# Eight more products into an unread bank behind each group of the relation pass

## The reference

```python
def _L2_gnn_ref(h, W, bias_term, gate_weight, gate_bias, loop_weight, src, dst, rel):
    loop_message = h @ loop_weight
    xw = jnp.einsum('ni,rio->rno', h, W)
    msg = xw[rel, src] + bias_term[rel]
    gw = gate_weight[..., 0]
    gate = jax.nn.sigmoid(jnp.sum(msg * gw[rel], axis=-1) + gate_bias[rel, 0])
    agg = jax.ops.segment_sum(msg * gate[:, None], dst, num_segments=n_nodes)
    node_repr = agg + loop_message
    return jax.nn.relu(node_repr)

x = _layernorm(x + _L0_gnn_ref(x, edge_index, ...))   # attention
x = _layernorm(x + _L1_gnn_ref(x, edge_index, ...))   # MLP
x = _layernorm(x + _L2_gnn_ref(x, ..., src, dst, edge_type_8))
x = _layernorm(x + _L3_gnn_ref(x, edge_index, ...))   # attention
```

## Time and profile before

| | us |
|---|---|
| median of three runs | 5380.08 |
| the profiled execution | 5375.34 |
| its span, from first to last instruction | 5373.5 |
| relation pass, first to last gather start | 2856.8 to 4030.5 |
| first attention pass, the same | 51.5 to 1251.7 |
| MLP pass, the same | 1335.0 to 2547.6 |
| second attention pass, the same | 4087.9 to 5286.7 |

### The profile page before, as it was taken

The page is one execution under the profiler, slowest core; times in us unless marked ns, Lnnn a source line. Parts: engine busy times, 40 slices in busy tenths (PEclk is TensorE's granted clock), DMA queues, the critical chain, the costliest instruction groups (busy, mean ns, idle before and its releaser), DMA issues. The chain is left out here.

```text
span 5373.5 us, 52586 instructions
## 1 busy us (share of the span) xinstructions
PE 3031.7 (56%) x15318; PEld 2725.6 (51%) x15318; DVE 2583.0 (48%) x5261; ACT 1435.2 (27%) x3816; POOL 3188.7 (59%) x3353
## 2 busy tenths in 40 slices
PE   2667676666477777777663232323322566666665
PEld 2566566665466666666631232322322556655665
DVE  2354444545477777777772121111212355554555
ACT  0010010101488888888651000000000011111111
POOL 5666666662666666666015666666664666666662
PEclk6556666656798888898876566666665655555656
DMA  5333333332333333333033111121112333333331
GB/s 126 86 104 101 99 97 101 101 95 69 99 102 101 102 101 102 102 101 101 4 141 101 44 50 49 47 51 49 51 49 65 86 97 95 100 98 95 99 98 50
DMA packets 254435, 458.48 MB, mean 85 GB/s; under 512 B 105399, under 2 KB 153912, under 8 KB 254136
## 3 DMA queue, kind: packets, MB, share of 16 engines
q0 software_dynamic: 119808, 280.51, 20.3%
q1 hardware_dynamic: 127272, 169.92, 9.7%
q10 hardware_dynamic: 7056, 4.56, 0.3%
HBM read 411.70 MB, written 43.03 MB: 85 GB/s over the span
## 5 line engine op out<-in xcount | busy, mean ns | idle before, releaser
L881 POOL DMA_INDIRECT rows<-gat_table,src_i x1664 | 1576.8, 948 | 840.3 <-issue 470.5
L1561 POOL DMA_INDIRECT rows<-mlp_table,src_i x832 | 788.8, 948 | 507.1 <-issue 306.4
L1293 POOL DMA_INDIRECT rows<-rel_table,rel_i x832 | 787.0, 946 | 443.0 <-issue 298.3
L1168 PE MATMUL p_sum<-rows,hot 128*128 128x133 f32 x3328 | 783.2, 424 | 36.6 <-issue 18.3
L1160 PEld LDWEIGHTS p_adc<-adw,hot_t 128*128 128x128 f32 x3328 | 659.4, 303 | 275.8 <-DVE hot_t L919 252.1
L1160 PE MATMUL p_adc<-adw,hot_t 128*128 128x8 f32 x3328 | 658.3, 336 | 233.3 <-DVE hot_t L919 218.5
L1168 PEld LDWEIGHTS p_sum<-rows,hot 128*128 128x128 f32 x3328 | 733.0, 325 | 38.7 <-DVE rows L945 20.4
L1450 PE MATMUL p_sum<-hot,rows 128*128 128x128 f32 x1664 | 305.8, 350 | 709.1 <-DVE hot L1320 419.4
L1722 PE MATMUL p_sum<-hot,rows 128*128 128x128 f32 x3328 | 510.9, 326 | 334.3 <-issue 302.5
L1722 PEld LDWEIGHTS p_sum<-hot,rows 128*128 128x128 f32 x3328 | 490.7, 238 | 376.1 <-issue 340.1
L1450 PEld LDWEIGHTS p_sum<-hot,rows 128*128 128x128 f32 x1664 | 281.9, 260 | 734.3 <-DVE hot L1320 437.1
(11 more groups left out here) (262 smaller groups left out, 3869.0 us busy)
## 6 DMA issues: line engine op xcount, KB each, us to landing
drow<-in_dst_rows SPq DMA_DIRECT2D x208, 512.0 KB
rows<-gat_table,src_i POOLq DMA_INDIRECT x1664
rel_table<-tab SPq DMA_DIRECT2D x49, 512.0 KB, 2.6
rows<-mlp_table,src_i POOLq DMA_INDIRECT x832
eat<-in_edge_t SPq DMA_DIRECT2D x104, 128.0 KB
rows<-rel_table,rel_i POOLq DMA_INDIRECT x832
gat_table<-tab SPq DMA_DIRECT2D x23, 274.0 KB
mlp_table<-tab SPq DMA_DIRECT2D x11, 512.0 KB
```

The lines of the kernel that those rows point to most:

```text
L881: pool.indirect_dma_start(out=rows[:, n % RING, t, :], out_offset=None, in_=net.gat_table[:, :], in_offset=bass.IndirectOffsetOnAxis(ap=ne ...
L1168: end = nc.tensor.matmul(p_sum[:, 0:SUMS], hot[:, n % HALF, t, :], rows[:, n % RING, t, 0:SUMS], start=(t == 0), stop=(t == T - 1))
L1293: pool.indirect_dma_start(out=rows[:, n % RING, t, :], out_offset=None, in_=net.rel_table[:, :], in_offset=bass.IndirectOffsetOnAxis(ap=ne ...
L1561: pool.indirect_dma_start(out=rows[:, n % RING, t, :], out_offset=None, in_=net.mlp_table[:, :], in_offset=bass.IndirectOffsetOnAxis(ap=ne ...
```

## The change

A constant `FILL = 8` is added, and a PSUM tensor `p_idle`. Behind the eight products of each group, after the one that raises `summed`, PE multiplies `FILL` times the identity and one tile of the group's one-hot, each product by itself, into `p_idle`, which nobody reads. No wait and no signal is added.

```diff
+FILL = 8
@@ rel_pass
         p_iota = s.ps("p_iota", [P, P])
+        p_idle = s.ps("p_idle", [P, 512])
         px = s.ps("px", [P, UNIT, P])
@@ add_up(n) on TensorE
                 for t in range(T):
                     end = nc.tensor.matmul(p_sum[n % 2][:, 0:P], rows[:, n % RING, t, :], hot[:, n % HALF, t, :], start=(t == 0), stop=(t == T - 1))
                 end.then_inc(s.summed, 1)
+                for t in range(FILL):
+                    nc.tensor.matmul(p_idle[:, 0:P], net.ident[:, :], hot[:, n % HALF, t, :], start=True, stop=True)
```

## The result

The changed kernel takes 5406.55 us, the median of five runs (5398.31 to 5411.24), against 5380.08 for the kernel before (5378.63 to 5388.16, five runs too). The ratio is 1.0038 with an interval of 1.0027 to 1.0050: slower, by 20 us on the ratio and by 26 us on the medians. The profiled execution took 5399.78 us with a span of 5398.0; before it was 5375.34 and 5373.5. So 24.5 us of span are to be explained.

A forecast was written before the change was run, and what follows sets the result against it. The prediction took the relation pass to be bound by POOL's gathers and their debt, not the products. +14 us in the pass and +6 in the tail gave +20, forecast 5400 us (+0.37%), range 5362 to 5442 us.

The forecast's parts named there:

- What bounds the pass: Relation pass: the gathers' pace on POOL with its debt sets the time, not the products; PE idle for 70%.
- The debt line: POOL's stops beyond the usual 0.30 us: about 0.147 us for each gather of the run plus 0.45 us per stop.
- Runs of 16 in place of 32: Relation pass: with fill, POOL stops after about 16 gathers instead of 32, 52 stops in place of 30.
- +14 in the pass: Relation pass: more POOL stops cost +14 us, taken between +10 and +22; bounds -13 and +39.
- +6 in the tail: After POOL's last gather: five groups +0.9 us each, some +4.5, and the last fill +1.8; taken as +6 us.
- The clock at 0: Middle of the relation pass: denser PE work raises the granted clock from 0.62 to 0.7 or more, worth 0 us.
- (d): Rival: a faster clock shortens each of 30 catch-ups by 1.5 us, giving 5335 us; chance 0.06.
- The bank: `p_idle` in PSUM: nothing waits for it or reads it, no wait is added, 0 us.
- (a): Rival: POOL stops at every group, 1.459 us a gather, +39 us and +10 in the tail, 5429 us; chance 0.20.
- (b): Rival: all hidden in the pass, runs stay at 24 to 32, only the tail costs, 5384 us; chance 0.27.
- (c): Rival: products behind the group push its late signal out, POOL stops less; up to 134.5 us, 5246 us; chance 0.06.
- (e): Rival: unread products might vanish or the clock not rise; the latter leaves the sum as is; no chance given.

The follow-up runs named there:

- six_b: Kernel before the change with six gathers per group instead of eight in the relation pass, output wrong; first to last gather there took 890.4 us against 1173.7.
- fill2: The changed kernel with two products of fill per group instead of eight; ratio 1.0005 to the kernel before the change.
- fill16: The changed kernel with sixteen products of fill per group instead of eight; ratio 1.0128 to the kernel before the change.
- half_b: Kernel before the change with relation-pass gathers of 64 rows instead of 128, output wrong; first to last gather there took 1182.1 us.
- paced_b: Kernel before the change with two 128x1 POOL memsets ahead of each gather in all passes, no fill; 5406.3 us, ratio 1.0044.
- ring16_b: Kernel before the change, no fill, with sixteen slots instead of eight in the relation pass's ring `rows`; 5438.4 us, ratio 1.0042.
- narrow: The changed kernel with its eight fill products cut to 8 columns moved and 32 loaded; ratio 1.0032 to the kernel before the change.
- Tailoff: The changed kernel without fill behind the last eight groups; ratio 1.0022 to the kernel before the change.

## Why the prediction was right, step by step

**What bounds the pass.** Held. PE's busy time in the pass nearly doubled, and the pass is still 831 intervals of 1.25 us and the stops, 1038.8 + 149.0 = 1187.8.

**The debt line.** 0.147 us a gather and 0.45 a stop were read from stops of other passes. For after it gives 122.3 + 0.45 x 51 = 145.3 us and 149.0 were found, for six_b 110.6 and 112.8, for fill2 with its 36 true stops 138.5 and 140.1. It falls short in fill16 (155.6 for 179.0) and in half_b, whose gathers are shorter. It describes the sum well. As a rule for a single stop it doesn't hold (after 8 gathers 0.46 to 7.30 us in after), and its 0.45 for a stop fell with paced_b. The prediction read the debt as something that POOL outruns and that needs 1.397 us a gather; that this isn't the transfers is shown by the empty windows of ring16_b.

**Runs of 16 in place of 32.** Held in kind: 24 of 51 runs have 16 gathers, none has 32, and 51 waits are close to the 52 that I put. The argument was that about 64 records get through at a stop. Counting matmul records of the windows over the whole pass per wait supports it: 1696 x 1.1737 / 34 = 59 before, 2069 x 1.1774 / 42 = 58 in fill2, 3102 x 1.1882 / 51 = 72 in after, 72 in fill16, 82 in narrow, while PE's records per us rise from 1.7 to 4.4. Some waits are too short to delay a gather; by intervals over 1.35 us there are 29 stops before, 36 in fill2, 51 in after, 74 in fill16 and 46 in narrow, and the records per stop are 69, 68, 72, 72 and 80. The deeper ring, which left the runs at 32, speaks for it too, since it changes no record. It isn't exact: six_b has 49.

The Trainium skill, "TensorE: Matmul & The Clock Gate", section "Architectural detail", has the queue of 64 that I weighed. The trace doesn't bear out the size. There the prediction counted matmuls and weight loads together (32 records of fill and 32 of a group are one group of after), and counted so, 116 to 144 get through per wait in before, fill2 and after. Only the matmuls alone come near 64. No run here shows a queue as such.

**+14 in the pass.** Measured +14.5, but the working behind it is doubtful. I priced 22 more stops at 0.45, which is +10, and went up toward the runs of 16 as seen. The trace has 17 more waits, or 22 more stops if those that delay no gather are left out (51 for 29). By the debt line they are worth 7.7 or 9.9 us, half or two thirds of what was found. And paced_b shows that the number of stops isn't what is charged. The line over instructions gives 3328 more of them (1664 matmul records and as many weight loads) x 4.15 ns = 13.8 us, from rows that I had in front of me. I used the MLP and attention passes there only as bounds. So the term came out right by luck in part: the price was too small, and a guess upward mended it.

**+6 in the tail.** Measured +6.3. Timeline of PE in after's tail:

```profile
4053.04 1.95 PE L1452 MATMUL p_sum<-hot,rows 128*128 128x128 f32 x16
...
4061.87 1.95 PE L1452 MATMUL p_sum<-hot,rows 128*128 128x128 f32 x16
...
4065.88 1.95 PE L1452 MATMUL p_sum<-hot,rows 128*128 128x128 f32 x16
...
4070.39 1.95 PE L1452 MATMUL p_sum<-hot,rows 128*128 128x128 f32 x16
...
4074.28 1.95 PE L1452 MATMUL p_sum<-hot,rows 128*128 128x128 f32 x16
```

The groups here are 4.0, 4.5 and 3.9 us apart where I had 2.7 before, so each is +1.2 to +1.8, not +0.9. There are also six of them, not five, and they begin 4.0 us after POOL's last gather (4049.0), not 8.9. The last real record starts 27.0 us after POOL's last gather, where it was 22.6. That is +4.4, as my +4.5 for the groups, but it is the sum of an earlier start, one more group and dearer groups. So the size of this term is luck in part too. Tailoff, with 55.5 us, shows that the tail's growth goes away with the fill of the last eight groups.

**The clock at 0.** The direction was right and the size too small in one place. I expected a granted clock of 0.7 or more in the pass, and it rose from 0.62 to 0.68; at 0.76, in fill16, the kernel is slowest. The stops got no shorter with it, so rival (d) is out: after 24 gathers 4.58 us against 4.35. In the tail the clock is worth something, by narrow's 3.78 against 1.95 us for one group. I had left that out because the tail looked warm before, in a window of 2.5 us; its first two groups took 6.44 us where after's take 1.95 and 2.05.

**The bank.** 0, as put: no wait in after names `p_idle`.

**The rivals.** (a), a stop at each group, is what fill16 approaches (53 runs of 8, 1.465 us a gather), not eight products. (b) is excluded by the stretch of +14.5 and by the ring. (c), that the signal only lacks work behind it, is refuted on all four bases: with more behind each group the waits rose (34 to 51, 30 to 46, 31 to 51, 29 to 48). (d) see above. (e) is out: 3102 records in place of 1696.

**The signs I named.** More than 34 waits: 51. Last gather 10 to 25 us later: 18.5, or 14.5 from the same start. Stops after 16 at about 3.3: 24 of them, 18 within 3.1 to 3.4 us and the others from 1.0 to 2.5. Records doubled. Clock at 0.7: missed, 0.68. None of the three signs against it appeared, but the one on stops after 32 gathers couldn't, as after has no run of 32; in fill2 the nine of them are 5.6 us and more.

**What stays open.** What charges 0.16 us to each gather beyond its 1.25, why an instruction of any engine adds to it, and why PE's records come singly for most of a run. The page shows how instructions are supplied, as packets of a DMA queue; these are its rows of before and of after:

```profile
q8 instruction: 128, 2.10, 0.2%
...
q8 instruction: 141, 2.31, 0.2%
```

With the fill's 3328 instructions there are 13 more packets of 16 KB, and 26 more in fill16 (154). Such a supply would fit the cost of an instruction. But it doesn't explain the debt itself: in the long stop of ring16_b the DMA engines are at 0.00 for 17 us, and POOL still waits. So a supply that the engines share with the gathers remains argued, and the late signal is one more thing that it would have to account for.

## What to carry to other kernels

Filler on an engine that is idle 70% of the time isn't free: here each product that nobody reads cost some 17 ns (14.5 us / 832) of the pass that another engine bounds, and the higher clock that it bought was worth nothing in the pass, where the stops go by the gathers. Before warming an engine, look in the waits for a row that a shorter product would end sooner. And where several passes share one bound, put their pace against their instructions: here a line through two passes of the kernel before gives the changed one within 0.5 us, better than a count of its stops, though it was drawn only afterwards and misses other kernels by 3 us and more.

## What the runs showed of the hardware

- Indirect gathers from POOL start every 1.25 us but keep up only one per 1.41 over a pass. Halving their rows took the instruction from 0.947 to 0.901 us and left 32 of them at 45.32 us with their stop, against 45.36.
- What POOL waits for in a stop isn't data: in ring16_b's stop of 23.11 us all engines are idle and the DMA share is 0.00 for 17 us, and the add that starts at 3110.40 belongs to a product whose records are over by 3030.5.
- Behind a stop some sixty PE records run back to back, 16 in 1.95 to 3.62 us, while POOL already issues gathers again (3444.02 in after). Then they come singly, 0.7, 1.4 or 2.1 us apart with nothing waited for (3464.56, 3466.65), until 4 us into the next stop.
- The 0.30 us between two gathers hides one memset of 0.12 us or two of 128x1 on the same engine (interval 1.25 to 1.26). With two, POOL pauses by itself, up to 1.51 us with nothing waited for.
- Instructions of any engine beside streaming gathers cost some 3 to 5 ns each of their pace, PE's and POOL's alike (fitted to the passes, above).
- An fp32 product of 32 loaded and 8 moved columns took 0.04 us a record where the granted clock was 1.00 (16 in 0.67) and 0.06 where it was 0.50 (16 in 1.02). The full one with 128 of each took 0.12 (16 in 1.95) and 0.24 (16 in 3.78 to 3.79).
